# A two-layer transformer on one core: the stage between the attentions written as a pipeline over chunks, the shared expert's weights loaded earlier, and the experts' totals summed by TensorE

## The reference

```python
out = jnp.einsum('bte,fe->btf', out, out_proj_weight)          # layer 0 attention, output projection
...                                                            # residual add and layer norm between the layers
kc = conv_general_dilated(x, Wconv, window_strides=(3,))       # layer 1 attention: a key for every third token
k_tmp = jnp.concatenate([x[:, :1, :], kc], axis=1)
q = x @ Wq.T;  k = k_tmp @ Wk.T;  v = k_tmp @ Wv.T
...                                                            # masked softmax attention, output projection
scores = jax.nn.sigmoid(xf @ gate_w + bias)                    # layer 1 feed-forward: 8 experts, the best 2 per token
top_scores, top_idx = jax.lax.top_k(scores, K)
up = jnp.einsum('th,ehi->tei', xf, up_w) + up_b
eo = jnp.einsum('tei,eih->teh', gelu(up), down_w) + down_b
combined = jnp.einsum('teh,te->th', eo * 0.1, w)
shared = (gelu(xf @ sw_up + sb_up) @ sw_down + sb_down) * 0.1  # an expert that every token passes
out = (shared + combined)
out = out / (jnp.max(jnp.abs(out), axis=-1, keepdims=True) + 1e-06)
```

## Time and profile before

| | us |
|---|---|
| median of 3 runs | 1303.87 |
| lowest, highest | 1302.8, 1305.22 |
| profiled execution, its own time | 1305.71 |
| profiled execution, its span | 1304.0 |
| PE busy (share of the span) | 1127.9 (86%) |
| DVE busy | 971.5 (75%) |
| ACT busy | 740.4 (57%) |
| POOL busy | 509.9 (39%) |
| SP's queue q1, share of 16 DMA engines | 26.4% |

### The profile page before, as it was taken

One profiled execution on the slowest core, in us unless ns is written; L12 is line 12 of the kernel. 1 busy time (PEld: TensorE's weight loads), 2 busy tenths in 40 slices (PEclk: granted clock), 3 DMA queues, 4 the chain that ended last, 5 costly groups with the idle time before them and its releaser, 6 DMA issues. The chain is left out here.

```text
span 1304.0 us, 22545 instructions
## 1 busy us (share of the span) xinstructions
PE 1127.9 (86%) x7455; PEld 619.1 (47%) x7458; DVE 971.5 (75%) x2126; ACT 740.4 (57%) x1143; POOL 509.9 (39%) x778
## 2 busy tenths in 40 slices
PE   4768879999999999999996755799999969999983
PEld 2436653444333434443433433444444438888862
DVE  8979978788888888888842533777777646777788
ACT  3657531666666656665664322166656557777762
POOL 6002220323233323332212526176666661566663
PEclk9889995999999999999987776599999989999997
DMA  4322970013121213120000121012222153678452
GB/s 130 97 79 68 129 85 18 26 38 126 34 75 50 91 35 99 38 94 27 2 2 1 54 76 44 23 48 64 58 64 63 38 178 110 189 235 241 152 130 65
DMA packets 94975, 103.51 MB, mean 79 GB/s; under 512 B 17217, under 2 KB 72838, under 8 KB 94864
## 3 DMA queue, kind: packets, MB, share of 16 engines
q1 hardware_dynamic: 88928, 93.09, 26.4%
q0 software_dynamic: 4992, 8.48, 1.9%
q10 hardware_dynamic: 944, 0.54, 0.2%
HBM read 64.67 MB, written 38.43 MB: 79 GB/s over the span
## 5 line engine op out<-in xcount | busy, mean ns | idle before, releaser
L1112 ACT ACTIVATE a_probs<-a_pst 128x1024 f32<-128x1024 f32 (+4 forms) x544 | 414.4, 813 | 284.5 <-PE a_pst L1060 284.0
L1136 DVE TENSOR_REDUCE a_tops<-a_ps 128x1 f32<-128x512 f32 (+9 forms) x624 | 341.4, 590 | 92.4 <-PE a_ps L1030 84.1
L976 POOL TENSOR_SCALAR_AFFINE_SELECT a_probs<-a_probs 128x256 f32<-128x256 f32 (+3 forms) x384 | 179.8, 480 | 387.3 <-ACT a_probs L1112 382.6
L1030 PE MATMUL a_ps<-kp,qp 96*128 96x512 bf16 (+9 forms) x1280 | 292.8, 307 | 0.8 <-DVE a_tops L1136 0.4
L1060 PE MATMUL a_pst<-qp,kp 99*128 99x512 bf16 (+4 forms) x1088 | 260.7, 332 | 22.6 <-DMA qp<-a_top_rows 18.9
L1079 PE MATMUL a_po<-a_probs,vh 128*32 128x512 f32 (+4 forms) x2176 | 233.1, 501 | 2.0 <-POOL a_probs L976 1.9
L1136 DVE TENSOR_REDUCE a_tops_lead<-a_ps 128x1 f32<-128x512 f32 x256 | 161.8, 683 | 5.7 <-PE a_ps L1030 5.4
L1027 PE MATMUL a_ps<-mask_s,identb 128*128 128x128 bf16 (+8 forms) x624 | 144.3, 234 | 7.0 <-PEq L1220 4.5
L1030 PEld LDWEIGHTS a_ps<-kp,qp 96*128 96x128 bf16 x1280 | 111.9, 101 | 79.1 <-DVE a_tops_lead L1136 15.3
L1060 PEld LDWEIGHTS a_pst<-qp,kp 99*128 99x128 bf16 (+1 forms) x1088 | 92.1, 100 | 120.1 <-ACT a_probs L1112 48.4
L1678 POOL DMA_INDIRECT chosen_rows<-e_slot_y,e_slot_x x92 | 93.4, 1015 | 87.9 <-DVE e_slot_y L1866 60.3
(11 more groups left out here) (269 smaller groups left out, 1715.7 us busy)
## 6 DMA issues: line engine op xcount, KB each, us to landing
e_slot_w<-weight_parts SPq DMA_DIRECT2D x23, 1024.0 KB
weight_parts<-a_cut SPq DMA_DIRECT2D x18, 512.0 KB, 3.1
qp<-q_parts SPq DMA_DIRECT2D x64, 96.0 KB
slot_rows<-empty_row SPq DMA_DIRECT2D x4, 1495.0 KB, 27.3
e_slot_x<-slot_rows SPq DMA_DIRECT2D x23, 260.0 KB, 5.4
a_raw<-in_wraw SPq DMA_DIRECT2D x18, 256.0 KB, 3.7
qp<-q_parts SPq DMA_DIRECT2D x64, 64.0 KB
q_parts<-o SPq DMA_DIRECT2D x24, 128.0 KB
```

What stands on the lines that cost most here:

```text
L976: pool.affine_select(out=seen, in_=seen, compare_op=ALU.is_ge, fill=0.0, base=m0, pattern=[[0, 2], [1, mw]], channel_multiplier=-1 if laye ...
L1030: last = pe.matmul(bank[:, i * room:i * room + w], sb["qp"][slot][0:KROWS, j, f["qt"] * P:(f["qt"] + 1) * P], sb["kp"][slot][0:KROWS, j // ...
L1112: act.activation(probs[local % RING][0:st["rows"], 2 * part:2 * part + 2, st["off"]:CHUNK], p_st[part][0:st["rows"], :, st["off"]:CHUNK], ...
L1136: dve.tensor_reduce(out, scores, AX.X, ALU.max).then_inc(s["banks_read"], 1)
```

## The change

Three things.

The stage between the attentions becomes a pipeline: a step `i` of every engine works on chunks at different places of their way (chunk i+4 is transposed, i+3 projected, i+2 added, i+1 normalised, i gets its queries), with no loop instruction. The bf16 parts are cut by TensorE and ACT: ACT writes a part out of the bank (`head_q`, `rest_q`), TensorE takes it off the bank by a product with minus the identity (`take_off_q`). The transposed, normalised chunk goes straight to `big`, the normalised one straight to `rows`, and the attention's output is transposed where it lies; the copies on DVE and ACT go. Each query buffer waits for its own store. SP loads only head group 0's operands inside the stage, after batch 1's stores; group 1's follow at the start of the attention, groups 2 and 3 after the rows of units 0 and 1.

The shared expert's weights are loaded at the end of the second attention, into a buffer of their own.

In `experts` POOL's adds go. A chunk's shared rows are transposed into a bank that stays open, and TensorE adds the two experts' rows by products with the identity (`add_rows`, and a third for chunks 0 and 1). DVE finishes two chunks at a time out of the banks, in the order FINAL. Results go to `big`, so no store is waited for.

```diff
+def load_shared(sp, io, sb, dram):
+
+    for i in range(2):
+        sp.wait_ge(sb["counts"]["experts"][f"cut_stored{i}"], START + 16 * CUTS // 2)
+    shared_in = sb["landed"]["shared"]
+    sp.dma_start(sb["shared_b"][:, :], io["wbias"][EXPERTS, :, :]).then_inc(shared_in[0], 16)
+    for c in range(2):
+        sp.dma_start(sb["shared_w"][:, 2 * c:2 * c + 2, :].rearrange("p a h -> p (a h)").bitcast(F32),
+                     dram["weights"][2 * EXPERTS + c, :, :]).then_inc(shared_in[c], 16)
+
...
+                load_operands(sp, sb, dram, layer, geo.keys, 0, 1)
+                for par in range(2):
+                    sp.wait_ge(sb["counts"]["between"][f"q_stored{par}"], START + STORES * CHUNKS // 2)
...
+                    if layer == 1 and n + 2 < GROUPS:
+                        load_operands(sp, sb, dram, layer, geo.keys, 0, n + 2)
...
+            if layer == 1:
+                load_shared(sp, io, sb, dram)
...
+        TURN, PROJECT, ADD, NORMALISE = 4, 3, 2, 1
+        steps = range(-TURN, CHUNKS + 2)
...
-            def chunk(following, n, b, c, more=False):
-                if following is not None:
-                    root(following)
-                pool.wait_ge(s["q_copied"], START + n + 1)
-
-                wait_apart(pool, s["q_stored"], START + STORES * (2 * b), sb["passed"])
-                split_parts(pool, qf[:, :], rest[:, :], q_parts[c][:, :, :], s["split_steps"], START + 4 * n,
-                            sb["passed"])
-                pool.wait_ge(s["split_steps"], START + 4 * n + 4)
...
-            store_q1(sp, sb, dram, 0, 0)
-            store_q1(sp, sb, dram, 0, 1)
...
-            for g in range(GROUPS):
-                load_operands(sp, sb, dram, 1, KEYS1, 0, g)
-            with sp.Fori(1, B - 1) as b:
-                store_q1(sp, sb, dram, b, 0)
...
+            for b in range(B):
+                for c in range(2):
+                    if 2 * b + c < CHUNKS - 1:
+                        store_q1(sp, sb, dram, b, c)
+                if b < B - 1:
+                    store_k1(sp, sb, dram, b)
+                if b == 1:
+                    for par in range(2):
+                        sp.wait_ge(s[f"q_stored{par}"], START + STORES)
+                    sp.wait_ge(s["k_stored"], START + STORES)
+                    load_operands(sp, sb, dram, 1, KEYS1, 0, 0)
...
+            def take_off_q(n, part, copied):
+                pe.wait_ge(s[copied], START + n + 1)
+                pe.matmul(p_q[n % 2][:, :], sb["minus_identb"][:, :], q_parts[n % 2][:, part, :], start=False, stop=True,
+                          skip_group_check=True).then_inc(s["rests_done"], 1)
...
+            for i in steps:
+                if is_chunk(i):
+                    turn_xn(i)
+                if is_chunk(i - 1):
+                    take_off_q(i - 1, 0, "heads_done")
+                if ended(i) is not None:
+                    convolve(ended(i))
+                if lagged(i) is not None:
+                    take_off_k(lagged(i), 0, "k_heads_done")
+                if is_chunk(i + PROJECT):
+                    project(i + PROJECT)
+                if is_chunk(i):
+                    query(i)
+                    route(i)
+                if is_chunk(i - 1):
+                    take_off_q(i - 1, 1, "middles_done")
+                if ended(i) is not None:
+                    keys_values(ended(i))
+                if lagged(i) is not None:
+                    take_off_k(lagged(i), 1, "k_middles_done")
+                if is_chunk(i + TURN):
+                    turn_o(i + TURN)
```

```diff
+            def head_q(n):
+                act.wait_ge(s["q_projected"], START + n + 1)
+                if n >= 2:
+                    act.wait_ge(s[f"q_stored{n % 2}"], START + STORES * (n // 2))
+                act.activation(q_parts[n % 2][:, 0, :], p_q[n % 2][:, :], ACT.Copy).then_inc(s["heads_done"], 1)
+
+            def rest_q(n, part, copied):
+                act.wait_ge(s["rests_done"], START + 2 * n + part)
+                act.activation(q_parts[n % 2][:, part, :], p_q[n % 2][:, :], ACT.Copy).then_inc(s[copied], 1)
...
-                act.activation(xnt[:, c * CHUNK:(c + 1) * CHUNK], p_xn[:, :], ACT.Copy).then_inc(s["xnt_copied"], 1)
-                act.activation(sb["rows"][:, bass.ds(n * CT, CT), 0:E], xn[:, :].rearrange("p (t e) -> p t e", e=E),
-                               ACT.Copy).then_inc(s["rows_kept"], 1)
-                act.wait_ge(s["q_projected"], START + n + 1)
-                act.wait_ge(s["split_steps"], START + 4 * n)
-                act.activation(qf[:, :], p_q[:, :], ACT.Copy).then_inc(s["q_copied"], 1)
...
+            def add(n):
                 dve.wait_ge(s["projected"], START + n + 1)
...
+            def normalise(n):
                 dve.wait_ge(s["root_steps"], START + 2 * n + 2)
                 dve.wait_ge(s["moment_steps"], START + 6 * n + 6)
...
+            for i in steps:
+                if ended(i) is not None:
+                    logits(ended(i))
+                if is_chunk(i + NORMALISE):
+                    normalise(i + NORMALISE)
+                if is_chunk(i + ADD):
+                    add(i + ADD)
+                if ended(i) is not None:
+                    choose(ended(i))
...
+        FINAL = [2, 3, 0, 4, 1, 5, 6, 7]
+        RES = 5
+        FINISH_AT = {HT * (JOBS - 1) + 1: 0, HT * JOBS: 1}
+        TURN_AT = {HT * (EARLY + n + SLOT_TILES + 2): EARLY + n for n in range(3)}
+        TURN_AT.update({HT * JOBS: 5, HT * JOBS + 2: 6, HT * (JOBS + 1): 7})
+        ADD_AT = {HT * (JOBS - 2) + 1: 0, HT * (JOBS - 2) + 3: 1, HT * (JOBS - 1) + 1: 2, HT * (JOBS - 1) + 3: 3,
+                  HT * JOBS + 1: 4}
...
-            sp.dma_start(shared_b[:, :], io["wbias"][EXPERTS, :, :]).then_inc(shared_in[0], 16)
-            for c in range(2):
-                sp.dma_start(shared_w[:, 2 * c:2 * c + 2, :].rearrange("p a h -> p (a h)").bitcast(F32),
-                             dram["weights"][2 * EXPERTS + c, :, :]).then_inc(shared_in[c], 16)
...
-            for n in range(CHUNKS):
-                pool.wait_ge(chosen_in[n // 2], 2 * 16 * TOPK)
-                tiles = slice(n * CT, (n + 1) * CT)
-                pool.tensor_tensor(picked[0][:, tiles, :], picked[0][:, tiles, :], picked[1][:, tiles, :], ALU.add)\
-                    .then_inc(s["pairs_added"], 1)
-                pool.wait_ge(s["pairs_added"], START + n + 1)
-                pool.wait_ge(s["rows_done"], START + shared_job(n) + 1)
-                pool.tensor_tensor(acc[:, tiles, :], acc[:, tiles, :], picked[0][:, tiles, :], ALU.add)\
-                    .then_inc(s["totals_added"], 1)
...
+            def turn_total(n):
+                at, j = FINAL.index(n), shared_job(n)
+                pe.wait_ge(s["sums_read"], START + j + 1)
+                bank_free(at)
+                for t in range(CT):
+                    last = pe.matmul(p_total[at % 4][:, t * P:(t + 1) * P], sums[j % 2][:, t * P:(t + 1) * P],
+                                     sb["ident"][:, :], start=t == 0, stop=False, is_transpose=True,
+                                     skip_group_check=True)
+                last.then_inc(s["y_turned"], 1)
+
...
+                else:
+                    pe.wait_ge(s["res_ready"], START + CT * (at - 3))
...
+            def add_rows(at):
+                n = FINAL[at]
+                tiles = slice(n * CT, (n + 1) * CT)
+                whole = p_total[at % 4][:, :].rearrange("p (t e) -> p t e", e=E)
+                if n < EARLY:
+                    bank_free(at)
+                    pe.wait_ge(s["rows_done"], START + n + 1)
+                    pe.matmul(whole, sb["ident"][:, :], acc[:, tiles, :], start=True, stop=False, skip_group_check=True)
+                if at % 2 == 0:
+                    pe.wait_ge(chosen_in[at // 2], 2 * 16 * TOPK)
+                for i in range(TOPK):
+                    last = pe.matmul(whole, sb["ident"][:, :], picked[i][:, tiles, :], start=False, stop=i == TOPK - 1,
+                                     skip_group_check=True)
+                last.then_inc(s["totals_added"], 1)
...
+                step, base = s["res_steps"], RES * pair
+                total = [p_total[at % 4][:, :].rearrange("p (t e) -> p t e", e=E) for at in (2 * pair, 2 * pair + 1)]
+                for i in range(2):
+                    dve.wait_ge(s["totals_added"], START + 2 * pair + i + 1)
+                    dve.tensor_reduce(top[:, i * CT:(i + 1) * CT], total[i], AX.X, ALU.max, apply_absolute_value=True)\
+                        .then_inc(step, 1)
+                dve.wait_ge(step, START + base + 2)
...
+                for i in range(2):
+                    n = FINAL[2 * pair + i]
+                    for t in range(CT):
+                        dve.scalar_tensor_tensor(res[:, n * CT + t, :], total[i][:, t, :], inv[:, i * CT + t:i * CT + t + 1],
+                                                 X[:, n * CT + t, :], ALU.mult, ALU.add).then_inc(s["res_ready"], 1)
```

338 lines of the change are left out of this document (165 added, 173 removed).

## The result

| | before | after |
|---|---|---|
| median, us | 1304.55 | 1252.94 |
| lowest, highest | 1302.8, 1306.5 | 1250.26, 1255.12 |
| profiled execution, its span | 1304.0 | 1253.2 |

The ratio is 0.9603, with a 95% interval of 0.9579 to 0.9627: 51.6 us less, where 30 were forecast (1274, range 1261 to 1293).

The account below looks back on a forecast made before the run. Bound: TensorE, over 90% busy nearly everywhere, but a chain through all engines between the attentions. Stage -29, second attention +6.5, shared weights -0.5, end of experts -7 make -30 off 1303.87: 1274 us, range 1261 to 1293.

Parts of the forecast that it names:

- The stage, -29: Stage between the attentions: the pipeline and moved loads shorten it from 126.8 to 98 us.
- the prediction's 98: Stage between the attentions: its forecast length in us, 92.6 at the priced clocks plus 5.3 for slow clock.
- slow-clock allowance: Stage, steps 0 to 5: half of the 10.7 us they would lengthen at granted clock 0.78, 5.3.
- the sign "over 0.85": Stage between the attentions: a granted TensorE clock over 0.85 would show the forecast right.
- Steps 0 to 5 with their coupling: Stage, after a prologue of 12 us: steps sum to 37.8, coupling adds 2.3, step 6 begins at 52.
- The first rival: Stage and last adds: TensorE stays at 1.2 GHz, stage -2, end +14, 1322 us in all; chance 0.04.
- lower bound of -34: Stage between the attentions: the largest gain stated, with no slow stretch.
- The second attention, +6.5: Start of the second attention: group 1's late loads delay unit 1's fills; 6.5 us longer, bounds +4 and +10.
- The experts, -7.5: Experts: early shared weights give -0.5; the end, without POOL's adds and with something lost between pairs, -7.
- four (end gives nothing): End of the experts: no gain, since TensorE takes on 15.3 us there; 1281 us; chance 0.12.
- Two (stores pace every step): Stage: waits for query stores lose 2 to 3 us a step, eight steps give 20 back; 1294 us; chance 0.12.
- Three (late loads free): Second attention: group 1's wait is taken out of later unit waits, costing nothing; 1267 us; chance 0.1.

Follow-up runs that it names:

- the shallow pipeline: The kernel after with pipeline distances 2, 1, 1, 0 in place of 4, 3, 2, 1: 1262.8 us, 0.9683 of before.
- the experts' part: The kernel before with only the change in `experts` and the early loading of shared weights into their own buffer: 1287.1 us, 0.9872.
- the pad ahead: The kernel before with 32 unused bytes a partition allocated ahead of the attention's operand buffers: 1297.4 us, again 1296.2.
- the stage's part: The kernel after with `experts` and the loading of its shared weights as before: 1265.7 us, 0.9711 of before.
- the kernels with pads: The kernel before with 32 unused bytes ahead of the operand buffers, behind them, or both: 1297.4 (again 1296.2), 1300.7 (again 1300.4) and 1297.2 us.
- the third buffer together with the loads' place: The kernel after with three query-part buffers and head groups 0 and 1 loaded in small blocks between the stage's stores: 1234.9 us, 0.9468 of before.

## Why the prediction was wrong in size

Of the 20.8 us of span between forecast and result, 11.7 lie in the stage, 6.2 ahead of it, 1.6 in the second attention and 1.3 in the experts. The mechanism of the stage was right and its terms were too large; the first attention had no term at all.

**The stage, -29 against -40.7: terms mis-sized on the side of caution.** Counted from the first attention's last result, the prediction's 98 is 98.9, against 87.0.
- The slow-clock allowance, "I take half, 5.3", was not needed beside the other terms. The clock is 1.00 from 716 to 745, where TensorE's only waits are 0.33, 0.60 and 0.94. It is low in the prologue and behind the long wait, which the sum had mostly priced low already, and 0.74 from 703 to 716, which it had not. Over the whole stage it is 0.79 (0.69 before), so the sign "over 0.85" did not come, though the time was shorter than forecast.
- Steps 0 to 5 with their coupling: 37.4 came of 40.1, and in it two errors stand against each other. Steps 0 and 1 took 13.7 where 10.3 had been summed, with slow products and a wait of 2.84 for `x`. Steps 2 and 3, at the high clock, took 12.1 where 15.0 had been summed: the prediction gave each group of products the whole length of its row, but the next group starts before the row ends. In the kernel after the query row is 1.02 long, and the router's products start 0.86 behind its start; theirs is 0.95 long, and the next one starts after 0.81 (rows below). For the end of the experts the prediction had counted the right way (0.85 in a stream). With the steps, chunk 4's store came earlier: the wait ended 66.3 behind the last result, forecast 69.9: 3.6.
- From there to the end 23.7 had been forecast without the allowance, 20.7 came, 3.0: the ranks took 2.05 at the high clock, where the 3.9 of the earlier trace rows were at the low one, and the choice and keys of batch 3 ran closer together.

5.3, 3.6 and 3.0 are the 11.9. The rows on the products, TensorE in the kernel after:

```profile
721.48 1.02 PE L1326 MATMUL b_pq<-big,wq 128*128 128x512 f32 x2
722.34 0.95 PE L1337 MATMUL b_pv<-gw,big 128*128 128x8 f32 x8
723.15 0.38 PE L1344 MATMUL b_pq<-q_kept,minus_identb 128*128 128x512 bf16 x1
```

The first rival rested on small idles between groups of products (the Trainium skill's "TensorE: Matmul & The Clock Gate", section "A second HAM failure mode: psum-queue depth-cycling"). From 716 to 745 the trace does not show what that section describes: 1.00. But there are only three idles in it, so this says little about the rule. In the shallow pipeline, where each step has a wait of up to 4.2, the clock is 0.87 from 718 to 745 and the stage 10.7 longer; how much of that is clock and how much the waits themselves was not taken apart. The rival's -2 was also added wrongly: its own terms, 92.6, 29 and 6, make 128, about 1 above the 126.8 of before. It changes nothing, as the rival fell.

The stated lower bound of -34 was wrong as a bound: it took the slow clock out, and none of the other terms. Several terms had each been taken on the slow side, and the range had no case in which all of them are too large.

**Up to the first attention's end, 0 against -6.2.** No step of the prediction looked at it, since no instruction there changed; it stood in the sum at nothing. 0.7 lies ahead of the attention and 5.5 in it. In the kernel before the place of the buffers alone does this: the experts' part, or 32 unused bytes, takes the attention from 508.7 to between 503.0 and 503.9, and the pad ahead gives 6.3 and 7.8 in the medians. In the kernel after the place is worth 2.3. The other 3 come with the stage's part, which moves none of these buffers and stands behind that attention (505.7 with it alone). Why they do, and how the place works, is not shown. The Trainium skill's "DMA: Bandwidth & Descriptors", section "How a descriptor splits into AXI transactions", has a rule for descriptors that do not start 256-byte aligned: the first read starts at the boundary below. Counted by the sizes of the buffers ahead of it, `qp` starts at a multiple of 256 neither before nor after, so by that rule both pay, and it does not tell the two apart. The runs do.

**The second attention, +6.5 against +4.9.** The mechanism was right (unit 1's fills wait 5.97 us for `kp`). Its price is about 5: the first unit's result stands 29.4 to 30.3 behind the first product in the three kernels with late loads and the buffers of after, 24.4 to 25.1 in the five without. Groups 2 and 3 came in time, as forecast. The second attention also gains from the new places (229.8 to 225.9 with the experts' part alone), so the +4.9 of the table is a sum of two things and near the forecast partly by luck; and this one execution holds 3.6 more, lost in units 3, 10 and 11, counted from 0, which two other kernels with late loads and the same places don't show (230.1 and 230.2).

**The experts, -7.5 against -8.8.** Start: right, and for the reason given (TensorE waits 6.81 for VectorE's split). End, from the landmark of the earlier trace rows (1216.75 after): 42.9 before, 36.5 after, -6.4. The terms had added up to 35.3, and 35.9 was forecast with the loss between pairs. TensorE was 0.4 later than summed and VectorE 0.7 more: both maxima of the last pair stand behind the eight scalings of the pair before, where the sum had one. Between the experts' first product and the landmark 1.9 went as well, which no term had. The experts' part alone takes it out too (2.0); the kernels with pads have 0.3 to 0.9 of it. What in that part does it was not tested.

**The rivals.** One (slower) and four (end gives nothing) fell. Two (stores pace every step) was true in small: ScalarE waits 20.9 us in five places for query stores, of which 12.15 is the forecast wait, and the third buffer together with the loads' place takes 12.2 out of the stage (87.0 to 74.8). Three (late loads free) fell: they cost about 5.

## What to carry to other kernels

Price products that follow each other by the distance from start to start, not by the length of a row. Keep a case in the range in which all cautious terms are wrong together. Where one queue carries both loads and stores, look at what each block of loads is put in front of, and count the issuing queue itself among the engines that a barrier waits for. Before the place of instructions is credited or blamed for a change in a part that they don't touch, move the buffers by 32 bytes and time that.

## What the runs showed of the hardware

- A move of buffers by 32 bytes, no instruction changed: operand buffers that DMAs write at a multiple of 64 instead of 32 past it, 1297.2 against 1304.0 (0.995, 0.9938 to 0.9962); the small buffers behind them from 0 to 32 past it, 1300.4 (0.9976, 0.9967 to 0.9985).
- An operand load costs SP 0.6 to 0.8 us of issue each; 24 in a row, 17.4 us, kept SP busy for 8.4 us after VectorE, the last engine at work, had finished, and TensorE's wait at the barrier was 13.31 in place of 4.45.
- TensorE's granted clock was 1.00 over 29 us with waits of at most 0.94, and 0.51 in the 12 us behind a wait of 9.83.
